# Two-layer image kernel: norms stored as overlapping strips, fewer unit loads, one store per band, residual products dealt round

## The reference

```python
def _L1_conv_ref(x, spatial_weight):
    patches = _extract_patches(x)                 # 25 shifted copies
    dot = jnp.einsum('bchw,bckhw->bkhw', x, patches)
    norm_x = jnp.sqrt(jnp.sum(x * x, axis=1))
    norm_p = jnp.sqrt(jnp.sum(patches * patches, axis=1))
    sim = dot / jnp.maximum(norm_x[:, None] * norm_p, EPS)
    weight = (sim + 1.0) * 0.5 * spatial_weight[None, :, None, None]
    return jnp.einsum('bckhw,bkhw->bchw', patches, weight)

x = x + _L0_conv_ref(_gn(x), w0, w1, w2, bias)
x = x + _L1_conv_ref(_gn(x), spatial_weight)
```

## Time and profile before

| | |
|---|---|
| median of three runs | 2228.85 us |
| the profiled execution | 2231.01 us |
| its span, first to last instruction | 2229.3 us |
| mean TensorE clock granted | 0.885 of full |
| TensorE busy | 1737.3 us, 78% |
| VectorE busy | 1363.9 us, 61% |
| one round of the loop (image 3) | 252 us |
| start of the residual, from unit to unit, image 3 | 27.7, 24.6, 23.2, 21.4, 19.1, 30.7, 16.8 us |

### The profile page before, as it was taken

How to read it: one execution, slowest core, us unless ns; L and a number is a source line. 1 busy time by engine, 2 the same in 40 slices (tenths; PEclk the granted TensorE clock), 3 DMA queues, 4 the chain that set the end, 5 groups by cost and what they waited for, 6 DMA issues and landing times.

```text
span 2229.3 us, 53057 instructions
## 1 busy us (share of the span) xinstructions
PE 1737.3 (78%) x19007; PEld 988.9 (44%) x19007; DVE 1363.9 (61%) x1995; ACT 742.9 (33%) x1318; POOL 430.6 (19%) x760
## 2 busy tenths in 40 slices
PE   5776887978878787878778787878779787876576
PEld 3542344545444444535345344545345444443354
DVE  6427756756677456856577456755578465865453
ACT  2320243423333243423333243423333252423341
POOL 1343322012311123012310123012300224010000
PEclk7888897889989898989989898999989898987577
DMA  5243337552666337562656447552754447571555
GB/s 164 75 106 95 85 104 174 151 137 78 187 155 159 94 104 191 153 140 78 179 156 151 97 114 196 152 139 79 176 149 128 117 105 201 127 174 38 141 145 127
DMA packets 128073, 296.57 MB, mean 133 GB/s; under 512 B 44532, under 2 KB 77300, under 8 KB 127220
## 3 DMA queue, kind: packets, MB, share of 16 engines
q1 hardware_dynamic: 90864, 190.39, 33.5%
q0 software_dynamic: 36864, 101.47, 17.6%
HBM read 221.92 MB, written 69.83 MB: 131 GB/s over the span
## 4 chain that ended last, share of the span: by engine, by line
PE 41%; DMA 17%; DVE 15%; SPq 13%; issue 10%; ACT 2%; DVEq 1%; POOL 1%; ACTq 0%; POOLq 0%
PE conv L1274 11%; DMA unit_mem<-d_n 8%; DMA d_n<-st_n 8%; PE conv L1248 6%; PE gram L1339 5%; PE out_ps L1364 5%; PE out_ps L1375 3%; SPq L409 3%; PE conv L1233 3%; PE stat_ps L1297 3%; SPq L383 3%; SPq L402 2%; SPq L381 2%; PE vals_ps L1322 2%; PE conv L1484 2%
## 5 line engine op out<-in xcount | busy, mean ns | idle before, releaser
L1012 DVE SCALAR_TENSOR_TENSOR wgt<-gram,tapw 124x512 f32<-124x512 f32 x512 | 350.1, 685 | 476.9 <-PE gram L1339 441.2
L1274 PE MATMUL conv<-thl,wconv 128*128 128x496 f16 (+2 forms) x1920 | 535.5, 407 | 20.0 <-DVE xa L892 10.7
L454 POOL DMA_DIRECT2D ring<-in_x x576 | 334.1, 585 | 666.5 <-ACT xa L526 345.0
L1339 PE MATMUL gram<-unit_mem 128*60 128x128 f16 x4096 | 250.6, 247 | 210.1 <-DMA unit_mem<-d_n 137.9
L1339 PEld LDWEIGHTS gram<-unit_mem 128*60 128x60 f16 x4096 | 152.3, 113 | 420.0 <-issue 419.5
L1274 PEld LDWEIGHTS conv<-thl,wconv 128*128 128x128 f16 x1920 | 167.3, 103 | 215.3 <-issue 62.1
L1248 PE MATMUL conv<-thl,wconv 128*128 128x480 f16 (+7 forms) x1200 | 256.9, 368 | 0.0
L483 POOL DMA_DIRECT2D up<-d_z x128 | 68.5, 537 | 813.1 <-DVE xa L943 755.4
L1297 PE MATMUL stat_ps<-st_sq,sq_c 128*128 128x306 f32 x256 | 117.9, 549 | 125.5 <-DVE flag L993 40.4
L1375 PE MATMUL out_ps<-wgt,vals 124*32 124x128 f32 x4096 | 204.8, 296 | 0.8 <-DVE wgt L1012 0.4
L526 ACT ACTIVATE vals<-vals_ps 124x512 f32<-124x512 f32 x128 | 76.2, 596 | 341.3 <-PE vals_ps L1322 337.6
(11 more groups left out here) (137 smaller groups left out, 2110.8 us busy)
## 6 DMA issues: line engine op xcount, KB each, us to landing
unit_mem<-d_hl SPq DMA_DIRECT2D x128, 360.0 KB
unit_mem<-d_hl SPq DMA_DIRECT2D x256, 180.0 KB
ring<-in_x POOLq DMA_DIRECT2D x288, 128.0 KB, 3.4
ring<-in_x POOLq DMA_DIRECT2D x288, 127.0 KB, 3.7
d_hl<-st_hl SPq DMA_DIRECT2D x128, 180.0 KB
d_v<-st_v SPq DMA_DIRECT2D x128, 180.0 KB
unit_mem<-d_v SPq DMA_DIRECT2D x64, 360.0 KB
up<-d_z POOLq DMA_DIRECT2D x160, 128.0 KB, 4.9
```

What stands on the lines that cost most here:

```text
L454: pool.dma_start(dst, src).then_inc(raw_in[slot], 16)
L1012: V.scalar_tensor_tensor(out=dst, in0=g, scalar=SIM_SCALE ** 2, in1=tapw[:, :].unsqueeze(1).to_broadcast([KN, 2, 2 * QN]), op0=ALU.add, op ...
L1274: last = mm(dst[:, :, b0:b1], wconv0[:, w, 2 * (p % ROWS4) + s, dx + 2, :], thl[:, p % 2, d, s, :, b0 + dx:b1 + dx] if p % ROWS4 != 1 else ...
L1339: last = mm(bank[row:row + KQ, col:col + QN], key[:, q, e_at, TH * KW * g:TH * KW * g + KQ], tile[:, :, TH * g + 1:TH * g + 1 + TH, 1:1 + ...
```

## The change

Four things. (1) VectorE writes the norms as strips into st_s, of float32 and double-buffered, st_n is single; DRAM holds them strip by strip, and a load is two DMAs of one row. The wait for the save of two halves ago moves. (2) Keys are one DMA, queries two, over a source that is repeated. (3) A band is stored by one DMA. (4) The residual's loops are exchanged. Constants that follow from it (counts of semaphores, pads, the guarded branch) change with it.

```diff
-SAVES, LOADS = 80, 176
+SAVES, LOADS, BAND_STORES = 80, 96, 16
...
-        st_n = sb("st_n", [P, 2, UN], F32)
+        st_n, st_s = sb("st_n", [P, UN], F32), sb("st_s", [P, 2, FN], F32)
...
-        d_n = dram("d_n", [B, 2 * BANDS, Q, UN], F32)
+        d_n = dram("d_n", [B, 2 * BANDS, GROUPS, Q, SN], F32)
...
-                sp.dma_start(d_n[b, h], st_n[0:P:C, h % 2, :]).then_inc(half_saved[h % 2], 16)
+                sp.dma_start(d_n[b, h].rearrange("e q n -> q e n"), st_s[0:P:C, h % 2, :].rearrange("p (e n) -> p e n", e=GROUPS)).then_inc(half_saved[h % 2], 16)
...
-                for j in range(2):
-                    sp.dma_start(keys[s][2 * C * j:2 * C * (j + 1)].rearrange("c q e n -> c (q e n)"),
-                                 d_hl[b, u].rearrange("l c q n -> (l c) (q n)")).then_inc(unit_in[s], 16)
-                for j, hl in enumerate((0, 0, 1, 1)):
-                    sp.dma_start(queries[s][C * j:C * j + C].rearrange("c q e n -> c (q e n)"),
-                                 d_hl[b, u, hl].rearrange("c q n -> c (q n)")).then_inc(unit_in[s], 16)
+                sp.dma_start(keys[s].rearrange("p q e n -> p (q e n)"),
+                             d_hl[b, u].rearrange("(a l) c q n -> a (l c) (q n)", a=1).to_broadcast([2, 2 * C, Q * FN])).then_inc(unit_in[s], 16)
+                for hl in range(2):
+                    sp.dma_start(queries[s][2 * C * hl:2 * C * (hl + 1)].rearrange("p q e n -> p (q e n)"),
+                                 d_hl[b, u, hl:hl + 1].rearrange("l c q n -> l c (q n)").to_broadcast([2, C, Q * FN])).then_inc(unit_in[s], 16)
...
-                norms = d_n[b, u].rearrange("(a q) (h w) -> a (q h) w", a=1, w=SW)
-                for e in range(GROUPS):
-                    row = 64 + C * (e // 2)
-                    sp.dma_start(norm_strips[s][row:row + 1, e % 2].rearrange("a (n w) -> a n w", w=KW),
-                                 norms[:, :, TW * e:TW * e + KW]).then_inc(unit_in[s], 16)
+                for a in range(2):
+                    row = 64 + C * a
+                    sp.dma_start(norm_strips[s][row:row + 1].rearrange("p e n -> p (e n)"),
+                                 d_n[b, u, 2 * a:2 * a + 2].rearrange("(p e) q n -> p (e q n)", p=1)).then_inc(unit_in[s], 16)
...
-                for g in range(BANDS):
-                    row = 2 * (BH * r + TH * g)
-                    sp.dma_start(out[b, :, row:row + 2 * TH, :].rearrange("c h w -> c (h w)"),
-                                 ostage[C * g:C * g + C].rearrange("c h w -> c (h w)")).then_inc(stored, 16)
+                rows = out[b, :, 2 * BH * r:2 * BH * (r + 1), :].rearrange("c (g h) w -> g c (h w)", g=BANDS)
+                sp.dma_start(rows, ostage[:, :, :].rearrange("p h w -> p (h w)")).then_inc(stored, 16)
...
-                    act.wait_ge(half_saved[h % 2], START + SAVES * (4 * b + h // 2))
...
                     copy(st_b[:, :], st_a[:, :], func=ACT.Square).then_inc(root_squared, 1)
+                    act.wait_ge(half_saved[h % 2], START + SAVES * (4 * b + h // 2))
...
-                nc.scalar.activation(st_hl[:, 1, h % 2, 0:UN], st_n[:, h % 2, :], ACT.Sign, bias=edge[:, :], scale=-1.0,
+                nc.scalar.activation(st_hl[:, 1, h % 2, :], st_s[:, h % 2, :], ACT.Sign, bias=edge[:, :], scale=-EPS_SIM ** -0.5,
...
-                prep_chain.link(dve, V.scalar_tensor_tensor(out=sq, in0=sq, scalar=EPS_SIM ** -0.5, in1=st_a[:, :],
-                                                            op0=ALU.mult, op1=ALU.mult))
+                dve.wait_ge(half_saved[h % 2], START + SAVES * (4 * b + h // 2))
+                prep_chain.link(dve, V.tensor_tensor(in_strips(st_s[:, h % 2, :]), strips(st_n[:, :]), strips(st_a[:, :]), ALU.mult))
...
-                for g in range(BANDS):
-                    row = BH * r + TH * g
-                    for q in range(Q):
+                for q in range(Q):
+                    for g in range(BANDS):
+                        row = BH * r + TH * g
                         last = mm(o[C * g:C * g + C, q, :].rearrange("p (h w) -> p h w", h=TH), ident[:, C * q:C * q + C],
```

More of the change, by code:

```diff
@@ L78 @@
 START = 1
-SAVES, LOADS = 80, 176
+SAVES, LOADS, BAND_STORES = 80, 96, 16
 POINT_MM = 3 * K
 HOOKS = [0, 4, 8, 12, 15, 19, 23, 27, 2 * POINT_MM]
-PAD_EDGE = P * (SH + SW - 1)
+PAD_EDGE = P * (SH + GROUPS * KW - 1)
 PAD_INNER = P * SH
@@ L436, in _ @@
                 iteration(i - 1)
-            sp.wait_ge(stored, START + 4 * 64 * B)
+            sp.wait_ge(stored, START + 4 * BAND_STORES * B)
         @block.gpsimd
@@ L575, in result @@
                 if half == 0:
-                    act.wait_ge(stored, START + 64 * (4 * b + r))
+                    act.wait_ge(stored, START + BAND_STORES * (4 * b + r))
                 o = out_ps[:, :].rearrange("p (q h w) -> p q h w", q=Q, h=TH)
@@ L628, in norms @@
                     act.wait_ge(unit_vec, START + 8 * b + h)
-                    act.wait_ge(half_saved[h % 2], START + SAVES * (4 * b + h // 2))
                 copy(st_a[:, p * PIECE:(p + 1) * PIECE], stat_ps[:, 0:PIECE], func=ACT.Abs_reciprocal_sqrt,
                      bias=tiny[:, :])
-                copy(st_n[:, h % 2, p * PIECE:(p + 1) * PIECE], stat_ps[:, 0:PIECE]).then_inc(n2_kept, 1)
+                copy(st_n[:, p * PIECE:(p + 1) * PIECE], stat_ps[:, 0:PIECE]).then_inc(n2_kept, 1)
                 if p == 1:
@@ L954, in units_open, with units_refine @@
                 dve.wait_ge(root_squared, 8 * b + h + 1)
-                ch.link(dve, V.scalar_tensor_tensor(out=st_b[:, :], in0=st_b[:, :], scalar=-0.5, in1=st_n[:, h % 2, :],
+                ch.link(dve, V.scalar_tensor_tensor(out=st_b[:, :], in0=st_b[:, :], scalar=-0.5, in1=st_n[:, :],
                                                     op0=ALU.mult, op1=ALU.mult))
-            def units_refine(h):
-                sq = st_n[:, h % 2, :]
+            def units_refine(b, h):
                 prep_chain.link(dve, V.scalar_tensor_tensor(out=st_a[:, :], in0=st_b[:, :], scalar=1.5, in1=st_a[:, :],
                                                             op0=ALU.add, op1=ALU.mult))
-                prep_chain.link(dve, V.scalar_tensor_tensor(out=sq, in0=sq, scalar=EPS_SIM ** -0.5, in1=st_a[:, :],
-                                                            op0=ALU.mult, op1=ALU.mult))
+                dve.wait_ge(half_saved[h % 2], START + SAVES * (4 * b + h // 2))
+                prep_chain.link(dve, V.tensor_tensor(in_strips(st_s[:, h % 2, :]), strips(st_n[:, :]), strips(st_a[:, :]), ALU.mult))
             def image_of(h):
@@ L992, in set_flag @@
                 pads = PAD_EDGE if h // 2 in (0, BANDS - 1) else PAD_INNER
-                V.tensor_scalar(flag[:, h % FLAGS:h % FLAGS + 1], stat_ps[0:1, 0:1], 0.5, float(P * UN // 2 - pads), ALU.mult, ALU.add)\
+                V.tensor_scalar(flag[:, h % FLAGS:h % FLAGS + 1], stat_ps[0:1, 0:1], 0.5, float(P * FN // 2 - pads), ALU.mult, ALU.add)\
                     .then_inc(flag_done, 1)
@@ L1006, in weights @@
                 with dve.If(short_ones > 0):
-                    V.tensor_scalar(dst, guard_ps[0:KN, :].rearrange("p (t n) -> p t n", t=2), 1.0, None, ALU.min)
+                    V.tensor_scalar(dst, guard_ps[0:KN, :].rearrange("p (t n) -> p t n", t=2), 1 / EPS_SIM, 1.0, ALU.mult, ALU.min)
                     dve.drain()
@@ L1056, in iteration @@
                         units_open(b, h)
-                        units_refine(h)
+                        units_refine(b, h)
                         units_close(b, h)
@@ L1077, in iteration @@
                         alone(dve)
-                        short_ones = dve.value_load(flag[0:1, j % FLAGS:j % FLAGS + 1], min_val=0, max_val=P * UN)
+                        short_ones = dve.value_load(flag[0:1, j % FLAGS:j % FLAGS + 1], min_val=0, max_val=P * FN)
                     for k in range(PAIRS):
@@ L1437, in hook @@
                                 alone(pe)
-                                short_ones[0] = pe.value_load(flag[0:1, j % FLAGS:j % FLAGS + 1], min_val=0, max_val=P * UN)
+                                short_ones[0] = pe.value_load(flag[0:1, j % FLAGS:j % FLAGS + 1], min_val=0, max_val=P * FN)
                                 unit_here(b, j)
```

## The result

The changed kernel takes 3592.96 us (median of four, 3587.44 to 3597.89) where the kernel before takes 2233.94 beside it: ratio 1.607, 95% interval 1.599 to 1.616. It is slower by 61%. Forecast were 3918 us, with a range of 3500 to 4600.

A forecast was written before the change was run, and what follows sets the result against it. Before, TensorE nearly balances the save-load path; after, two DMA engines bound it: 298.8 us to the first save, seven images at 459 (3213), a last queue of 372, 36 to the end, less 2, give 3918 us; range 3500 to 4600.

The forecast's parts named there:

- Engines by the leading number: Key and query loads: engine count divides both patterns' leading numbers, so a source beginning with 2 gets two engines, not 16.
- Rival A: Key and query loads: count goes by destination alone or whole row number, so 16 engines stay; 2105 us, chance 0.12.
- rival B: Key and query loads: two engines per DMA, but a different two for each of the three; 2680 us, chance 0.04.
- The pace of an engine: Key and query loads on two engines: 21.75 GB/s each, from the tap masks' load, making 33.9 us per unit.
- Rival C: Key and query loads: two engines as forecast, but at 14.9 GB/s each, 15.5 us more per unit; 4910 us, chance 0.06.
- The queue: The two engines' work from an image's first save until load 7 lands: 403 us, then 56 to the next first save.
- The stretch after unit 7: Bare stretch at an image's end: grows by some microseconds as TensorE is often at 1.2 GHz; left out of the sum.
- The residual: Residual products on TensorE: 32 records take 1.14 us, saving 0.92 us per unit, 59 in all, reappearing as longer wait.
- The store: Band store on four engines at 89 GB/s: 5.9 us every second unit; only ScalarE's next band waits for it.
- The norms: VectorE's product goes from 796 to 898 ns, ScalarE's sign widens likewise: 0.1 us per unit each; moved waits cost zero.
- Rival A's sum: Gains if loads keep 16 engines: load waits, residual and ScalarE's waits, 125 us off 2231, giving 2105.
- The load waits: Within Rival A's sum, TensorE's 137.9 us of unit-load waits: 29 us less in unit 6, 46 off the other 51.

The follow-up runs named there:

- experiment 4: Kernel before with a one-row DRAM gap between high and low, so the keys' source is 2 x 32 rows without a repeat: 2830.60 us, ratio 1.263.
- experiment 5: Changed kernel with a channel's high and low rows side by side, queries' repeat second in the source, keys in two 64-row DMAs: 2166.17 us, 0.967 of before.
- experiment 7: Kernel before with only the residual's loops exchanged, its products dealt round: 2202.73 us, ratio 0.984.
- experiment 2: Kernel before with only the keys' and queries' DMAs changed to three over a source beginning with a repeat of 2: 3539.43 us, ratio 1.579.
- experiment 1: Changed kernel with the keys' and queries' six DMAs of before, on 16 engines; norms, store and residual as changed: 2162.78 us, 0.966 of before.
- Experiment 6: On top of experiment 5, DRAM laid out quadrant, channel, high/low, so saves are 128 rows on both sides, on 16 engines: 2039.92 us, 0.909 of before.

## Why the prediction was right, and by how much it was off

**Engines by the leading number: right.** Two engines at a share of 0.12 to 0.13, for all three DMAs. The saves had shown that a destination's number binds; experiment 4 shows that a source's does, without a repeat, and experiment 5 that the same repeat in second place costs nothing. By the Trainium skill's rule (DMA: Bandwidth & Descriptors, section Why a DMA increments its semaphore by 16 and not by 1) a source of 2 rows in front gives two engines, one of 32 over 64 gives 16, and 128 over 128 gives 16; the shares of 0.12, 0.99 and 0.94 agree. Rival A falls, and so does rival B, since the three DMAs together stay at two engines' share.

**The pace of an engine: mis-sized.** This term makes nearly all of the error. I took 21.75 GB/s from the load of the tap masks; the unit loads run at 26 when two engines carry them. 1,474,560 / 52,000 = 28.4 us in place of 33.9. With that, an image's 459 us become 415, and it took 422.3 (first saves at 727.09 and 1149.38):

```profile
727.09 1.34 SPq L381 DMA_DIRECT2D d_hl<-st_hl  x2
...
1149.38 1.33 SPq L381 DMA_DIRECT2D d_hl<-st_hl  x2
```

The total becomes 3918 - 64 x 5.5 = 3566, within 1% of 3593. The 26 GB/s were read from the changed kernel's trace, so this is a sum made afterwards, not a second forecast. Why the masks' rows of 12,800 bytes go slower per engine was not tried. Rival C's 14.9 GB/s is what 16 engines get together (226 to 243 GB/s in the windows shown); two don't meet that limit.

**The queue.** In image 1 load 7 is there at 1094.8 and the next image's first save at 1149.4: 54.6 us for the forecast's 56. From the first save to load 7 it is 367.7 for 403, of which the pace explains 44. The other terms were 9 us too small in sum. The stretch after unit 7 was to grow by some microseconds with the lower clock; it didn't.

**The residual: right.** In the changed kernel (chain in order of time) its 32 records take 1.01 us for the 1.14 forecast and the 2.06 of the earlier trace rows:

```profile
555.44 1.01 PE out_ps L1360 x32
556.45 0.44 PE out_ps L1371 x16
```

By experiment 7 TensorE saves 62.0 us for the 59 forecast, and the kernel before gains 35 to 40 of them (1.6%); rival A had 30. That it brings nothing in the changed kernel follows from the waits there and was not tried.

**The store: one wait not foreseen, and a pace too high.** I wrote that nobody waits but ScalarE's next band, two units later. In the changed kernel that wait is 355.6 us: the store is issued behind loads. TensorE waited only 6.3 us in all for ScalarE's copies into ostage, so little of it was passed on; what the store takes from the loads on the same engines is a part of the 54 us of experiment 2. The last store of all runs alone: from 3581 to 3587 the share is 0.24, the quarter that was forecast, but at 63 GB/s and not 89. So a store takes 8.3 us for the 5.9 forecast.

**The norms: right.** VectorE's product takes 908 ns for the 898 forecast. ScalarE's sign takes 891 ns for 801, the 0.1 us forecast. In the changed kernel the moved wait costs ScalarE 10.5 us in all, where the forecast put it at zero.

**Rival A's sum** gave 125 us for what is 77. The load waits were the wrong term: 75 us were to go, but of 137.9 experiment 1 still waits 129.9. Issuing a load in fewer and shorter steps hardly changed how long TensorE waited. The saves did: four engines, 8 us, in front of each load. Experiment 6 takes that away and with it all but 3.3 us of the wait, for 6% more.

## What to carry to other kernels

Before merging DMAs, read the leading number of both patterns: in every shape measured here a transfer got as many engines, up to 16, as divide both, and a repeat or a part number (2, 4) in front took 14 or 12 of 16 away, however many rows followed. A DMA share that stands at 0.25 or 0.12 can be a count of engines and not a low load. Lay DRAM out so that what is stored and what is loaded both begin with a number of rows that 16 divides (32, 64 and 128 here; the 124 rows of the tap masks got four engines). For the saves that was worth 6%, where two issues fewer per load, in experiment 5, were worth nothing.

## What the runs showed of the hardware

- Unit loads ran at 26 GB/s per engine on two engines and at 14.7 (235/16) on 16. Saves to DRAM show no such drop: 22 on four, and 333 GB/s at a share of 0.94 in experiment 6, which is 22 each. The band's store, on four, ran at 16 each (63 GB/s). What sets these paces was not tried.
- SyncE's issues are held up while the two engines are behind. In the changed kernel, issues that took 0.5 us before take several. The values' DMA does too, though it runs on all 16 (0.47 us in the earlier trace rows, 6.83 here):

```profile
546.20 0.62 SPq L398 DMA_DIRECT2D unit_mem<-d_hl  x1
546.94 9.50 SPq L401 DMA_DIRECT2D unit_mem<-d_hl  x2
556.54 6.83 SPq L403 DMA_DIRECT2D unit_mem<-d_v  x1
563.46 2.25 SPq L407 DMA_DIRECT2D unit_mem<-d_n  x2
```

  The likely reason, not tried by itself, is that an issue is over only when each of its engines has taken its part. So the chain's 55% of SyncE's lines are mostly time behind the two engines, not work in issuing.
- A second number of 2 that repeats its row (experiment 5) costs nothing that the windows or the time show.
